# Three units abreast instead of two in the opening of a fused LoRA and FFN kernel

## The reference

```python
w = weight[adapter_ids]
t = jnp.einsum('bsi,boi->bso', x, w)          # the first product
t = t.reshape(b * l, Dm)[:, perm].reshape(b * l, h, d)
t = jnp.einsum('bhd,hdm->bhm', t, up)         # up
t = jax.nn.gelu(t, approximate=False)
t = jnp.einsum('bhm,hmd->bhd', t, down)       # down
return x + t.reshape(b * l, h * d)[:, unperm].reshape(b, l, Dm)
```

## Time and profile before

| | |
|---|---|
| median of 3 runs | 297.74 us (297.6 to 298.1) |
| profiled execution: span | 296.1 us |
| profiled execution: time around its span | not listed apart; median less span is 1.6 us |
| TensorE busy | 290.6 us, 98% |
| VectorE, ScalarE, GpSimd busy | 179.2, 159.9, 98.8 us |
| granted TensorE clock, mean | 1.000 |
| moved by DMA | 77.87 MB, mean 263 GB/s |
| one whole unit of the first product | 5.62 us (start to start, units 2 to 3) |

### The profile page before, as it was taken

The page is one execution under the profiler, slowest core; times in us unless marked ns, Lnnn a source line. Parts: engine busy times, 40 slices in busy tenths (PEclk is TensorE's granted clock), DMA queues, the critical chain, the costliest instruction groups (busy, mean ns, idle before and its releaser), DMA issues.

```text
span 296.1 us, 4358 instructions
## 1 busy us (share of the span) xinstructions
PE 290.6 (98%) x1694; PEld 215.0 (73%) x1694; DVE 179.2 (61%) x211; ACT 159.9 (54%) x179; POOL 98.8 (33%) x92
## 2 busy tenths in 40 slices
PE   8999999999999999999999999999999999999994
PEld 7788888888888838886488855888468885444441
DVE  3599679589778455973658726685446523343333
ACT  5655453466764368344584265822853207777750
POOL 4000000068552007860527007702473405222234
PEclk9999999999999999999999999999999999999999
DMA  7999999999988947799576973876752864421335
GB/s 206 363 402 421 395 421 422 366 320 375 394 328 277 378 153 197 281 360 406 212 249 196 345 311 114 312 237 199 244 191 83 286 185 122 128 71 71 144 142 212
DMA packets 23699, 77.87 MB, mean 263 GB/s; under 512 B 2688, under 2 KB 11264, under 8 KB 18816
## 3 DMA queue, kind: packets, MB, share of 16 engines
q1 hardware_dynamic: 7056, 43.39, 39.3%
q0 software_dynamic: 7488, 25.18, 24.7%
q10 hardware_dynamic: 9136, 9.05, 8.8%
HBM read 60.82 MB, written 16.78 MB: 262 GB/s over the span
## 4 chain that ended last, share of the span: by engine, by line
PE 95%; DMA 2%; SPq 1%; POOL 1%; issue 0%; DVE 0%; ACT 0%; POOLq 0%; DVEq 0%
PE ps L641 38%; PE ps L645 19%; PE ps L698 19%; PE ps L674 6%; PE ps L677 5%; PE ps L680 5%; PE ps L606 2%; DMA w_raw<-w 2%; PE ps L611 1%; POOL out_late L319 1%; SPq L223 1%; SPq L251 0%; DVE w_raw L528 0%; ACT w_hi L429 0%; POOLq L361 0%
## 5 line engine op out<-in xcount | busy, mean ns | idle before, releaser
L641 PE MATMUL ps<-x_pair,w_hi 128*128 128x512 f32 x480 | 131.5, 395 | 0.0
L381 ACT ACTIVATE w_hi<-w_raw 128x1024 fp32r<-128x1024 f32 x58 | 58.3, 1056 | 62.8 <-PE ps L645 51.6
L415 ACT ACTIVATE hidden<-ps 128x1024 f32<-128x1024 f32 x64 | 61.6, 1028 | 55.1 <-PE ps L680 47.1
L641 PEld LDWEIGHTS ps<-x_pair,w_hi 128*128 128x128 f32 x480 | 82.0, 189 | 12.8 <-issue 1.8
L645 PEld LDWEIGHTS ps<-x_pair,w_lo 128*128 128x128 f32 x480 | 73.6, 189 | 10.2
L490 DVE TENSOR_TENSOR w_lo<-w_raw,w_hi 128x1024 fp32r<-128x1024 f32 x60 | 71.0, 1222 | 11.8 <-ACT w_hi L381 10.7
L645 PE MATMUL ps<-x_pair,w_lo 128*128 128x256 f32 x480 | 76.3, 281 | 0.0
L292 POOL DMA_INDIRECT t_raw<-y_rows,idx x32 | 34.9, 1090 | 115.1 <-DMA y_rows<-y_out 82.4
L518 DVE TENSOR_REDUCE y_out<-ps 128x256 f32<-128x512 f32 x64 | 42.8, 685 | 24.5 <-PE ps L645 23.0
L698 PE MATMUL ps<-hidden,down_sb 128*64 128x512 f32 (+1 forms) x264 | 57.4, 583 | 0.0
L510 DVE TENSOR_TENSOR t_lo<-t_raw,t_hi 128x512 fp32r<-128x512 f32 x32 | 21.7, 694 | 47.9 <-ACT t_hi L405 42.5
(11 more groups left out here) (29 smaller groups left out, 119.4 us busy)
## 6 DMA issues: line engine op xcount, KB each, us to landing
w_raw<-w SPq DMA_DIRECT2D x29, 1024.0 KB
y_rows<-y_out ACTq DMA_DIRECT2D x32, 256.0 KB
x_raw<-x_cols SPq DMA_DIRECT2D x7, 1024.0 KB
w_raw<-w SPq DMA_DIRECT2D x4, 256.0 KB, 5.0
w_raw<-w SPq DMA_DIRECT2D x2, 512.0 KB, 7.7
hidden<-up SPq DMA_DIRECT2D x1, 1024.0 KB, 12.3
down_sb<-down SPq DMA_DIRECT2D x1, 1024.0 KB, 12.3
w_raw<-w SPq DMA_DIRECT2D x2, 384.0 KB, 6.9
```

What stands on the lines that cost most here:

```text
L381: nc.scalar.activation(w_hi[:, g % WS, k, :], w_raw[:, g % WRAW, k, :], ACT.Copy).then_inc(w_hi_done, 1)
L415: nc.scalar.activation(hidden[:, f % HS, m, :, :], up_banks(f, m)[:, :, :], ACT.Gelu).then_inc(gelu_done, 1)
L641: nc.tensor.matmul(acc, w_hi[:, ws, k, col], x_pair[:, xs, k, :, :], start=(k == 0), stop=False)
```

## The change

`ABREAST = 3` takes the place of `PAIR` in all that concerns the opening. Units 0, 1 and 2 are each loaded, rounded and multiplied in the four pieces, in the order unit 0, 1, 2 of piece 0, then of piece 1 and so on. Unit 2's rounded weights lie in the tiles `up_hi` and `up_lo`. The unit that comes in two half loads, and is rounded into place 0 as unit 0 leaves it, is now the fourth (g = 3). From unit 3 on the place is (g − 3) % 2, so unit 4 has the one that unit 1 leaves. On ScalarE, `w_high(3)` goes (it is `fourth_w_high` now, in the same position as `third_w_high` was). On VectorE, `w_low(3)` stands where `w_low(2)` stood, ahead of `y_sum(0)`, and `w_low(g + 2)` behind `y_sum(g)` starts with g = 2. On SyncE, x of entry 1 follows the two half loads. The last piece of x of entry 0 is issued behind unit 2's third piece.

The same goes for the semaphores of the pieces, for the counts in the waits of `lora_unit` and GpSimd, and for the operands of the matmuls and of the pieces' roundings (`hi_of(g)` for `w_hi[:, g]`), which are left out below.

```diff
--- before.py
+++ after.py
@@ -34,6 +34,8 @@
+ABREAST = 3
+
 X_BY_ACT = 3
@@ -115,6 +117,10 @@
+
+        third_hi = up_hi.rearrange("p f m -> p (f m)").rearrange("p (k o) -> p k o", k=KT)
+        third_lo = up_lo.rearrange("p f m -> p (f m)").rearrange("p (k o) -> p k o", k=KT)
+
         up_raw = hidden[:, 0, :, :, :].rearrange("p m h t -> p (m h t)").rearrange("p (f m) -> p f m", f=FU)
@@ -213,9 +219,11 @@
-        def w_landed(g):
-
-            return 16 * (g // WRAW + (g % WRAW > PAIR))
+        def hi_of(g):
+            return w_hi[:, g, :, :] if g < PAIR else third_hi if g == PAIR else w_hi[:, (g - ABREAST) % WS, :, :]
+
+        def lo_of(g):
+            return w_lo[:, g, :, :] if g < PAIR else third_lo if g == PAIR else w_lo[:, (g - ABREAST) % WS, :, :]
@@ -225,16 +233,16 @@
-            def load_third_w(adapter):
+            def load_fourth_w(adapter):
                 for n in range(2):
                     k = slice(n * HALF, (n + 1) * HALF)
-                    sp.dma_start(w_raw[:, PAIR, k, :], w_rows(adapter, PAIR, k)).then_inc(third_w_in[n], 16)
+                    sp.dma_start(w_raw[:, ABREAST, k, :], w_rows(adapter, ABREAST, k)).then_inc(fourth_w_in[n], 16)
...
             def load_w(g, adapter):
-                if WRAW <= g < WRAW + PAIR:
+                if g < WRAW + ABREAST:
                     sp.wait_ge(first_w_lo[g - WRAW], PIECES)
-                elif g >= WRAW + PAIR:
-                    sp.wait_ge(w_lo_done, 2 * (g - WRAW - PAIR + 1))
+                else:
+                    sp.wait_ge(w_lo_done, 2 * (g - WRAW - ABREAST + 1))
                 sp.dma_start(w_raw[:, g % WRAW, :, :], w_rows(adapter, g % LPB, slice(0, KT))).then_inc(w_in[g % WRAW], 16)
@@ -251,13 +259,14 @@
             for n in range(PIECES):
-                load_first_w(0, n)
+                for g in range(ABREAST):
+                    load_first_w(g, n)
                 if n + 1 >= X_BY_ACT and n + 1 < PIECES:
...
                     sp.dma_start(x_raw[:, k, :], x_cols[0, :, k, :]).then_inc(first_x_in[n + 1], 16)
-                load_first_w(1, n)
-            load_third_w(adapter)
-            for g in range(PAIR + 1, NL):
+            load_fourth_w(adapter)
+            load_x(1)
+            for g in range(WRAW, NL):
                 if g % LPB == 0:
@@ -363,22 +372,23 @@
         def _(act):
-            def third_w_high(n):
-                act.wait_ge(third_w_in[n], 16)
+            def fourth_w_high(n):
+                act.wait_ge(fourth_w_in[n], 16)
...
                 k = slice(n * HALF, (n + 1) * HALF)
-                nc.scalar.activation(w_hi[:, PAIR % WS, k, :], w_raw[:, PAIR, k, :], ACT.Copy).then_inc(w_hi_done, 1)
+                nc.scalar.activation(hi_of(ABREAST)[:, k, :], w_raw[:, ABREAST, k, :], ACT.Copy).then_inc(w_hi_done, 1)
...
             def w_high(g):
-                act.wait_ge(w_in[g % WRAW], w_landed(g))
-                act.wait_ge(lora_done, OT * (g - WS + 1))
+                act.wait_ge(w_in[g % WRAW], 16 * (g // WRAW))
+
+                act.wait_ge(lora_done, OT * (PAIR if g == WRAW else g - WS + 1))
                 for n in range(2):
                     k = slice(n * HALF, (n + 1) * HALF)
-                    nc.scalar.activation(w_hi[:, g % WS, k, :], w_raw[:, g % WRAW, k, :], ACT.Copy).then_inc(w_hi_done, 1)
+                    nc.scalar.activation(hi_of(g)[:, k, :], w_raw[:, g % WRAW, k, :], ACT.Copy).then_inc(w_hi_done, 1)
@@ -436,11 +446,10 @@
                     first_x_high(n)
-                for g in range(PAIR):
+                for g in range(ABREAST):
                     first_w_high(g, n)
             for n in range(2):
-                third_w_high(n)
-            w_high(PAIR + 1)
+                fourth_w_high(n)
@@ -486,9 +495,9 @@
                 k = slice(n * HALF, (n + 1) * HALF)
-                dve.wait_ge(w_hi_done, 2 * (g - PAIR) + n + 1)
-                nc.vector.tensor_tensor(w_lo[:, g % WS, k, :], w_raw[:, g % WRAW, k, :],
-                                        w_hi[:, g % WS, k, :].bitcast(F32), ALU.subtract).then_inc(w_lo_done, 1)
+                dve.wait_ge(w_hi_done, 2 * (g - ABREAST) + n + 1)
+                nc.vector.tensor_tensor(lo_of(g)[:, k, :], w_raw[:, g % WRAW, k, :],
+                                        hi_of(g)[:, k, :].bitcast(F32), ALU.subtract).then_inc(w_lo_done, 1)
@@ -546,9 +555,9 @@
                     first_x_low(n)
-                for g in range(PAIR):
+                for g in range(ABREAST):
                     first_w_low(g, n)
-            w_low(PAIR)
+            w_low(ABREAST)
@@ -568,7 +577,7 @@
                         y_sum(g)
-                        if g % QUAD < 3 and 0 < g < NL - 2:
+                        if g % QUAD < 3 and PAIR <= g < NL - 2:
                             w_low(g + 2)
@@ -701,12 +710,12 @@
             for n in range(PIECES):
-                for g in range(PAIR):
+                for g in range(ABREAST):
                     first_lora_piece(g, n)
...
                 for g in lora_of(q):
-                    if g >= PAIR:
+                    if g >= ABREAST:
                         lora_unit(g)
...
```

More of the change, by code:

```diff
@@ L131, in build @@
         perm_in = sem("perm_in")
-        first_w_in = [[sem(f"first_w_in{g}_{n}") for n in range(PIECES)] for g in range(PAIR)]
+        first_w_in = [[sem(f"first_w_in{g}_{n}") for n in range(PIECES)] for g in range(ABREAST)]
         first_x_in = [sem(f"first_x_in{n}") for n in range(PIECES)]
         w_in = [sem(f"w_in{i}") for i in range(WRAW)]
-        third_w_in = [sem(f"third_w_in{n}") for n in range(2)]
+        fourth_w_in = [sem(f"fourth_w_in{n}") for n in range(2)]
         x_in = sem("x_in")
@@ L147, in build @@
         ones_set = sem("ones_set")
-        first_w_hi = [sem(f"first_w_hi{g}") for g in range(PAIR)]
-        first_w_lo = [sem(f"first_w_lo{g}") for g in range(PAIR)]
+        first_w_hi = [sem(f"first_w_hi{g}") for g in range(ABREAST)]
+        first_w_lo = [sem(f"first_w_lo{g}") for g in range(ABREAST)]
         first_x_hi = sem("first_x_hi")
@@ L305, in gather_late_rows @@
                 g = NL - WRAW + b // 2
-                pool.wait_ge(w_lo_done, 2 * (g - PAIR + 1))
+                pool.wait_ge(w_lo_done, 2 * (g - ABREAST + 1))
                 nc.gpsimd.indirect_dma_start(late_rows[:, b, :], None, x_late, block_rows(b)).then_inc(late_rows_in[b], 16)
@@ L428, in first_w_high @@
                 act.wait_ge(first_w_in[g][n], 16)
-                nc.scalar.activation(w_hi[:, g, k, :], w_raw[:, g, k, :], ACT.Copy).then_inc(first_w_hi[g], 1)
+                nc.scalar.activation(hi_of(g)[:, k, :], w_raw[:, g, k, :], ACT.Copy).then_inc(first_w_hi[g], 1)
             act.wait_ge(ones_set, 1)
@@ L539, in first_w_low @@
                 dve.wait_ge(first_w_hi[g], n + 1)
-                nc.vector.tensor_tensor(w_lo[:, g, k, :], w_raw[:, g, k, :], w_hi[:, g, k, :].bitcast(F32),
+                nc.vector.tensor_tensor(lo_of(g)[:, k, :], w_raw[:, g, k, :], hi_of(g)[:, k, :].bitcast(F32),
                                         ALU.subtract).then_inc(first_w_lo[g], 1)
@@ L605, in first_lora_piece @@
                     for k in ks:
-                        nc.tensor.matmul(y_bank(g, o), w_hi[:, g, k, col], x_pair[:, 0, k, :, :], start=(k == 0), stop=False)
+                        nc.tensor.matmul(y_bank(g, o), hi_of(g)[:, k, col], x_pair[:, 0, k, :, :], start=(k == 0), stop=False)
                 pe.wait_ge(first_w_lo[g], n + 1)
@@ L610, in first_lora_piece @@
                     for k in ks:
-                        last = nc.tensor.matmul(y_bank(g, o)[:, 0, :], w_lo[:, g, k, col], x_hi[:, 0, k, :], start=False, stop=(k == KT - 1))
+                        last = nc.tensor.matmul(y_bank(g, o)[:, 0, :], lo_of(g)[:, k, col], x_hi[:, 0, k, :], start=False, stop=(k == KT - 1))
                     if n == PIECES - 1:
@@ L617, in lora_unit @@
             def lora_unit(g):
-                b, ws = g // LPB, g % WS
+                b = g // LPB
                 xs = b % XS
@@ L638, in lora_unit @@
                         if o == 0:
-                            pe.wait_ge(w_hi_done, 2 * (g - PAIR) + n + 1)
+                            pe.wait_ge(w_hi_done, 2 * (g - ABREAST) + n + 1)
                         for k in ks:
-                            nc.tensor.matmul(acc, w_hi[:, ws, k, col], x_pair[:, xs, k, :, :], start=(k == 0), stop=False)
+                            nc.tensor.matmul(acc, hi_of(g)[:, k, col], x_pair[:, xs, k, :, :], start=(k == 0), stop=False)
                         if o == 0:
-                            pe.wait_ge(w_lo_done, 2 * (g - PAIR) + n + 1)
+                            pe.wait_ge(w_lo_done, 2 * (g - ABREAST) + n + 1)
                         for k in ks:
-                            last = nc.tensor.matmul(acc[:, 0, :], w_lo[:, ws, k, col], x_hi[:, xs, k, :], start=False, stop=(k == KT - 1))
```

(1 more changed line is left out.)

## The result

The changed kernel takes 299.04 us (median of 9 runs, 298.38 to 299.54) against 297.9 us for the kernel before; the ratio is 1.0034, 95% interval 1.0022 to 1.0047. It is slower by 1.1 us by the medians and by 1.0 us by the ratio. The profiled execution's own time is 299.26 us, its span 297.3.

A forecast was written before the change was run, and what follows sets the result against it. TensorE, busy 98% of the span, was taken to bound the kernel. The opening's −0.5 us and the later stall's +1.3 us gave +0.8 us on 297.74, so 298.5 us; range 297.6 to 299.4.

The forecast's parts named there:

- The opening: TensorE before unit 3: three units abreast cover part of the 1.34 us stall and win 0.5 us, bounds 1.2 and −0.1.
- The chain: VectorE and ScalarE links after unit 0's end make TensorE wait at unit 4: a new stall of 1.3 us.
- E: End of unit 0's last piece on TensorE, forecast at 19.63 against 16.60 before; the chain's times count from it.
- All of it hangs on E: If the opening runs better, unit 0's last piece ends earlier, and the end of the kernel with it, one for one.
- The cover at unit 5: Unit 5's low half is there 0.5 us before TensorE wants it, so no second stall.
- The queues: Later DMA issues, including unit 4's value read moved by about 1.5 us, fall into a backlog without emptying it: no cost.
- Rival E: Idle gaps let TensorE's clock fall, 5 us at 1.2 GHz: +2.5 us more, 301 us; chance 0.02.
- B: Same chain, but the opening's lateness at 9.18 does not return, front wins 1.0 to 1.2: 297.9 to 298.2; chance 0.23.
- C: Third unit's pieces late, 0.6 us more lost, or unit 5's room used up: 299.1 to 299.4 us; chance 0.14.
- D: VectorE's chain does not bind, so the front's gain of 0.5 to 1.2 stays: 297.2 to 296.5 us; chance 0.06.
- A: The forecast itself, unit 1's second piece 0.3 to 0.9 us late: 298.3 to 298.9 us; chance 0.55.
- The fixed part of a DMA: About 2.0 us per DMA; paid in a row, the added opening piece would cost 2.3 us instead of 0.47; judged not paid.

The follow-up runs named there:

- e8: The kernel of e6 with the down weights loaded behind unit 15's weights instead of behind unit 9's: 297.86 us, ratio 0.9993.
- e9: The kernel of e6 with both the early adapter read of e7 and the late down weights of e8: 297.63 us, ratio 0.9992.
- e3: The kernel before, two units abreast, with only VectorE's new order, both halves of w_low(3) ahead of y_sum(0): 298.94 us, ratio 1.0041.
- e5: The kernel before with x_high(1) ahead of y_park(0) on ScalarE and y_sum(2) ahead of x_low(1) on VectorE: 297.74 us, ratio 0.999.
- e10: The kernel before with the early adapter read of e7 and the late down weights of e8: 297.87 us, ratio 1.0.
- e6: The changed kernel with x_high(1) ahead of y_park(0) on ScalarE and y_sum(2) ahead of x_low(1) on VectorE: 299.03 us, ratio 1.0022.
- e0: The changed kernel run again, with no further change: 299.04 us, ratio 1.0057 to the kernel before.
- e7: The kernel of e6 with SyncE reading the adapter of entry 1 ahead of load_x(1): 297.66 us, ratio 1.0009.
- e1: The changed kernel with one move on ScalarE, x_high(1) ahead of y_park(0): 298.93 us, ratio 1.0057.
- e4: The changed kernel with opening pieces of 1, 1, 2 and 4 tiles instead of 1, 2, 2 and 3: 299.34 us, ratio 1.0058.

## Why the prediction was right

298.5 us and slower were forecast, 299.04 measured; the mechanism is the one forecast, and its size was a little low: +0.8 us forecast, +1.2 in the spans, +1.0 to +1.1 in the runs. The kernel before came out at 297.9 beside it, not at 297.74.

- The opening: a win of 0.5 us was forecast, 0.24 was had. The term that was off is the landing of unit 0's second piece. I let only unit 1's be late; with the new piece ahead of it unit 0's landed at 8.5 and TensorE, free at 8.74, took it at 9.29, 0.55 late, while unit 1's was then in time (9.84 on ScalarE, 10.77 on TensorE, against 10.45 forecast). Here the third unit did not cure the lateness of one piece; it moved it to the piece that is first in the second round. The other profiles agree: ScalarE rounds unit 0's second piece at 7.55 to 8.74 us with three units abreast and these pieces, at 6.97 to 7.34 with two, and TensorE waits for it in seven of those nine (not in e8 and e9).
- Whether the front won anything is open. Unit 3 starts at 24.32, 24.45, 23.95 and 23.63 in the four profiles with two units abreast (before, e3, e5, e10) and at 23.46 to 24.30 in the nine with three and these pieces. The 0.24 us lies within this spread. The wait of 0.42 us at unit 1's second piece, from which the forecast worked, is not there in e3, e5 or e10.
- The chain: every link came within 0.02 us of its forecast from E (19.88, forecast 19.63): x_high(1) at E + 5.43 (5.43), x_low(1) to E + 9.67 (9.67), y_sum(2) to E + 10.87 (10.87), the low weights at E + 12.01 (12.01). The stall was 1.4 us against 1.3; the difference is the 0.10 us between the end of the sum and TensorE's start.
- "All of it hangs on E": unit 5 started 0.34 us later than forecast (36.72 against 36.38), 0.25 of it from the later E and the rest from the link just named, as far as one execution can tell.
- The cover at unit 5 held: w_high(5) at 34.72 released by the sum, no wait of TensorE at 36.72.
- The queues, costed at nothing, were right by luck. The forecast said that the value read moves unit 4's load by about 1.5 us at no cost, as the DMA stream is a backlog. It moved by 0.7 us, to 18.7 (and to 20.2 in e6, whose SyncE program is the same), and the stream thinned: 303 GB/s from 20 to 21 us against 410 before, and 213 in e6. In the profiled execution that cost nothing: the first gather was issued at 61.50, 0.7 us later than before, and TensorE does not wait for it. In e0 the same hole is at 213 GB/s, the gather at 63.00, and still there is no wait; TensorE itself comes over 1 us late there, which may cover it (not tested). With the stall cut away, e6's median is no better than e0's. The sentence that failed is that later issue falls into a backlog without emptying it: the check was made on load_x(2) at 29 us, where it holds, and not on unit 4's load at 18 us.
- Rival E, the clock, did not come: the granted clock stayed at 1.00 through both new gaps. Rivals B, C and D did not either. The bare 299.04 lies between the ranges of A and C; against its own kernel before it is A's upper end (+0.6 to +1.2 us), and C's signs, a wait for the third unit's pieces or one at unit 5, are not in the trace.
- The fixed part of a DMA in the Trainium skill, "DMA: Bandwidth & Descriptors", section "Anatomy of one DMA": that section takes it from DMAs that GpSimd issues, and the added piece is issued by SyncE, so the estimate of 2.3 us was a loose one. The added piece moved unit 0's second landing from 7.15 to 8.52, 1.37 us, which lies between the 0.47 of the bytes and those 2.3; unit 1's moved by 0.6 (9.21 to 9.84). How much of this is bytes, a fixed part, or the half microsecond that SyncE takes for each issue (nine in 4.61 us), no run here separates. The 0.47 was too low for the piece right behind.

## What to carry to other kernels

When the opening of a pipeline is widened, follow the first result that now comes later, and write down on each in-order engine what stands behind its consumer. Here the low part of one weight unit, placed ahead of two sums, delayed a chain over two engines by 3 us, and it cost 1.1 us with the old opening and 1.4 with the new one. When a stall is removed, look at the next meeting point of the same streams, and at the spread of the runs before the median: one quick profiled execution said that all was well, while most runs were about 1 us slower or more. Compare a win of a few tenths with the same place in every profile at hand, not with one. Where a DMA stream is full for 45 us, ask of each load that moves whether the stream still holds: of the eleven profiles with the same loads, the three that moved the fewest bytes between 10 and 25 us were the three in which TensorE waited for a gather 50 us later. To read a value that names a load's source ahead of the wait before that load is cheap to try, but what it is worth here was not told from the noise.

## What the runs showed of the hardware

Reading one value for SyncE, a pointer and then the value, takes long under a full DMA stream. In e6:

```profile
L231 SPq TENSOR_LOAD <-ids_ptr x1: 1645/1645/1645, 16.2 to 16.2; - x1
...
L231 SPq TENSOR_LOAD <-ids x1: 1749/1749/1749, 18.0 to 18.0; - x1
```

That is 3.4 us; in the kernel before the same pair of reads took 1.38 us at the start of the span, 2.7 at 15 us, and 6.5 us at 27 us; in e7, moved ahead to 10.9 us, it took 5.3. And the 22 products of the warm-up (the 11 matmuls of `warm` are 22 instructions in the trace), the same in every kernel, took from 4.32 us (e1, e10) to 5.07 us (the changed kernel); the kernel before was at 4.97. What sets it was not tried. It hardly reaches the opening: where the warm-up was short TensorE waited behind it (0.85 us in e1, for the first low part of x), and its first product of the opening started at 6.11 to 6.58 us in all profiles but e4's (5.80).
